# First attention of a four-layer kernel: scores from 32-row operands, and the PSUM banks dealt out anew

## What is computed

```python
h = layernorm(x) * gamma + beta
q, k, v = heads(h @ w_qkv + b_qkv)                  # 16 heads, 8 dimensions each, 1024 tokens, batch of 4
scores = einsum('bhqd,bhkd->bhqk', q, k) / sqrt(8)
attn = softmax(scores, axis=-1)
out = einsum('bhqk,bhkd->bhqd', attn, v)
x = x + (residual + out @ w_out + b_out)
```

## Time and profile before

| what | value |
|---|---|
| median of 3 runs | 2992.23 us (2990.68 to 2992.49) |
| the profiled execution's own time | 2991.15 us |
| its span | 2989.4 us |
| busy share of the span | PE 95%, PE weight load 74%, DVE 78%, ACT 71%, POOL 60% |
| first maxima, first scores, last maxima, last scores start at | 24.1, 60.6, 871.0, 906.7 us |

### The profile page before, as it was taken

The page is one execution under the profiler, slowest core; times in us unless marked ns, Lnnn a source line. Parts: engine busy times, 40 slices in busy tenths (PEclk is TensorE's granted clock), DMA queues, the critical chain, the costliest instruction groups (busy, mean ns, idle before and its releaser), DMA issues.

```text
span 2989.4 us, 46698 instructions
## 1 busy us (share of the span) xinstructions
PE 2852.0 (95%) x16447; PEld 2209.1 (74%) x16447; DVE 2344.6 (78%) x4197; ACT 2124.2 (71%) x4692; POOL 1786.9 (60%) x1312
## 2 busy tenths in 40 slices
PE   6999999999999999999999999999999999999996
PEld 3555555555547777788888888888888888888885
DVE  8878888887777888778787777788777777877776
ACT  3776776777776555677777777777777777787773
POOL 5421521512104555578788787788778788777773
PEclk9999999999999999999999999999999999999997
DMA  1000000000012221000000000000000000000000
GB/s 47 9 16 9 16 9 9 16 9 15 9 49 75 84 84 57 8 1 1 1 1 3 1 3 3 1 3 3 3 1 3 3 1 3 3 1 3 3 3 6
DMA packets 28570, 42.70 MB, mean 14 GB/s; under 512 B 5097, under 2 KB 15913, under 8 KB 28337
## 3 DMA queue, kind: packets, MB, share of 16 engines
q1 hardware_dynamic: 28336, 39.72, 4.6%
HBM read 29.08 MB, written 2.23 MB: 10 GB/s over the span
## 4 chain that ended last, share of the span: by engine, by line
PE 72%; DVE 14%; issue 5%; POOL 5%; ACT 3%; DMA 0%; SPq 0%; DVEq 0%; POOLq 0%; ACTq 0%
PE P L1835 18%; PE P L1676 9%; PE P L1703 8%; PE P L1688 8%; PE P L1862 7%; PE P L1846 6%; PE P L1764 4%; DVE c_nm L1409 4%; DVE c_DT L1434 3%; PE P L1818 3%; PE P L1775 2%; PE P L1872 2%; PE P L1662 2%; POOL d_tn L1105 2%; POOL c_P L2073 2%
## 5 line engine op out<-in xcount | busy, mean ns | idle before, releaser
L1409 DVE TENSOR_REDUCE c_nm<-P 128x1 f32<-128x1024 f32 x512 | 624.3, 1219 | 299.8 <-PE P L1835 297.8
L914 ACT ACTIVATE c_P<-P,c_nm 128x1024 f32<-128x1024 f32 x512 | 573.5, 1120 | 250.9 <-DVE c_nm L1409 246.6
L1233 DVE TENSOR_REDUCE a_mx<-P 128x1 f32<-128x512 f32 x1024 | 641.0, 681 | 120.4 <-PE P L1676 119.7
L790 ACT ACTIVATE a_PT<-P 128x512 f32<-128x512 f32 x1024 | 531.6, 601 | 162.2 <-PE P L1688 160.9
L2073 POOL TENSOR_TENSOR c_P<-c_P,c_P 128x1024 f32<-128x1024 f32 (+1 forms) x256 | 623.1, 2434 | 21.4
L2071 POOL TENSOR_SCALAR c_P<-c_P,c_rr 128x1024 f32<-128x1024 f32 (+1 forms) x256 | 302.2, 1180 | 335.7 <-DVE c_rr L1421 335.7
L1862 PE MATMUL P<-c_DT,c_xkh 128*128 128x256 f32 x2048 | 453.1, 284 | 24.7 <-DVE c_Yl L1442 22.9
L1676 PE MATMUL P<-a_Kp,a_Qs 128*128 128x512 f32 x1024 | 427.5, 422 | 12.9 <-DVE a_mx L1233 5.7
L1688 PE MATMUL P<-a_Qs,a_Kp 128*128 128x512 f32 x1024 | 401.2, 395 | 3.1 <-DMA a_Qs<-a_mT 1.4
L1862 PEld LDWEIGHTS P<-c_DT,c_xkh 128*128 128x128 f32 x2048 | 351.2, 189 | 36.8 <-DVE c_Yl L1442 29.1
L1835 PE MATMUL P<-c_xth,c_Th 128*128 128x512 f32 x1024 | 363.9, 436 | 2.9 <-ACT c_P L914 2.9
(11 more groups left out here) (247 smaller groups left out, 5543.4 us busy)
## 6 DMA issues: line engine op xcount, KB each, us to landing
b_cwB<-cw_scratch SPq DMA_DIRECT2D x64, 256.0 KB, 5.4
a_Kp<-a_Kc SPq DMA_DIRECT2D x60, 128.0 KB, 2.4
c_stg<-in_cw SPq DMA_DIRECT2D x8, 640.0 KB, 4.7
a_Qs<-a_mT SPq DMA_DIRECT2D x256, 2.0 KB
...
```

The lines of the kernel that those rows point to most:

```text
L790: e.activation(m.PT[j][hs % 4][:, :], bank("scores", u, hs, j), ACT.Exp, scale=SCALE).then_inc(m.S["a_exp"])
L914: e.activation(m.P1[s][n % 4][:, :], P[:, k:k + 2, :].rearrange("p c k -> p (c k)"), ACT.Exp, bias=m.nm[:, n % 4, s:s + 1], accum_out=m.sm ...
L1233: e.tensor_reduce(m.mx2[u % 2][:, 16 * (t // 4) + 4 * j + t % 4, half:half + 1], bank("maxima", u, t, j, half), AX, ALU.max).then_inc(m.S[ ...
L1409: e.tensor_reduce(m.nm[:, n % 4, s:s + 1], P[:, k:k + 2, :].rearrange("p c k -> p (c k)"), AX, ALU.max, negate=True).then_inc(m.S["c_nm"])
```

## The change

- `scores` and `maxima` take the 32 partitions of one head alone. `a_Kp` and `a_Kc` become `a_Ks` (128 x 1024, three of them), and `zero`, the 32-row writes and SP's 4 DMAs per unit are gone. Unit 0's keys are written by one 128 x 512 operation each.
- Neighbours in PE's queue are of different heads: maxima go through heads 0, 1, 2, 3 and scores through 2, 3, 0, 1.
- Maxima have banks 0 to 3, with `values`, `divide` and `out_project`, which DVE reads. Scores have banks 5, 6, 7, with `turn_h`, `project`, `row2` and `turn_o`, which ACT reads (`RINGED_ACT`).
- LAG0 is 7: one step of s (8 slots) more between a unit's maxima and its scores.
- Hooks of `row2`, `divide`, `turn_o`, `out_project` and `values` move by 1 to 6 slots. `project` stays.

```diff
-LAG0 = 6
+LAG0 = 7
...
+RINGED_ACT = {"turn_h", "project", "row2", "turn_o"}
...
-    ring = Ring([3, 5, 6, 7])
-    st_ring = Ring([0, 1, 2])
+    ring = Ring([0, 1, 2, 3])
+    act_ring = Ring([5, 6, 7])
...
-        if step[0] in RINGED:
+        if step[0] in RINGED_ACT:
+            p.on([act_ring.take()], *step)
+        elif step[0] in RINGED:
...
-                hook(s0 + 19 + c, 3, "values", b + 1, c)
+                hook(s0 + 19 + c, 7, "values", b + 1, c)
...
-            hook(s0 + 4 + 4 * c, 2, "row2", u, c)
+            hook(s0 + 4 + 4 * c, 3, "row2", u, c)
...
-            hook(e0 + 5 + 4 * r, 1, "divide", u, r)
+            hook(e0 + 5 + 4 * r, 4, "divide", u, r)
             if gr == 3:
-                hook(e0 + 6 + 4 * r, 1, "turn_o", b, r)
-                hook(e0 + 7 + 4 * r, 1, "out_project", b, r)
+                hook(e0 + 6 + 4 * r, 7, "turn_o", b, r)
+                hook(e0 + 7 + 4 * r, 5, "out_project", b, r)
...
+            if um < NU:
+                t, half = (m % 4, m // 4) if um == 0 and m < 8 else (m // 2, m % 2)
+                on_ring("maxima", um, t, i % 4, half)
             if 0 <= ue < NU:
-                p.on([st_ring.take()], "scores", ue, m_e // 4, m_e % 4)
+                p.on([act_ring.take()], "scores", ue, m_e, (i + 2) % 4)
...
-        if wh:
-            w.wait_ge(*v.now("a_z", "project", u, wh, c))
-            for j in range(2):
-                r = slice(32 * j, 32 * j + 32)
-                e.tensor_tensor(m.Kp[0][r, j, cs], m.th[q][r, :], m.tq[q][r, :], ALU.add).then_inc(s)
-        else:
-            e.tensor_tensor(m.Qs[0][:, cs], m.th[q][:, :], m.tq[q][:, :], ALU.add).then_inc(s)
+        e.tensor_tensor((m.Ks if wh else m.Qs)[0][:, cs], m.th[q][:, :], m.tq[q][:, :], ALU.add).then_inc(s)
...
-            w.wait_ge(*at(f"a_kdma{u % 3}", "project", u, 1, 1))
+            w.wait_ge(*at("a_qs", "project", u, 1, half))
...
-        e.matmul(ps, m.Qs[u % 3][:, 128 * t:128 * t + 128], m.Kp[u % 3][:, j, 512 * half:512 * half + 512],
+        e.matmul(ps, m.Qs[u % 3][r, 128 * t:128 * t + 128], m.Ks[u % 3][r, 512 * half:512 * half + 512],
...
-        e.matmul(ps, m.Kp[u % 3][:, j, 128 * kt:128 * kt + 128], m.Qs[u % 3][:, 512 * c:512 * c + 512],
+        e.matmul(ps, m.Ks[u % 3][r, 128 * kt:128 * kt + 128], m.Qs[u % 3][r, 512 * c:512 * c + 512],
...
-            for j in range(4):
-                e.dma_start(m.Kp[u % 3][32 * j:32 * j + 32, j, :].bitcast(F32),
-                            m.Kc[u % 2][32 * j:32 * j + 32, :].bitcast(F32)).then_inc(S[f"a_kdma{u % 3}"], 16)
```

More of the change, by code:

```diff
@@ L136, in project_signals @@
     out = {"a_qk_pe": 1, "a_tq": 1}
-    if u == 0 and w == 1:
-        out |= {"a_first_dve": 4, "a_qs": 2}
-    elif u == 0 and c == 0:
+    if u == 0 and (w == 1 or c == 0):
         out |= {"a_first_dve": 3}
@@ L142, in project_signals @@
         out |= {"a_th": 2, "a_qs": 1}
-    if u and w and c:
-        out[f"a_kdma{u % 3}"] = 64
     return out
@@ L155 @@
 SIGNALS = {
-    "zero": {"a_z": 1},
     "one": {"a_z": 1},
@@ L310, in plan_all @@
         hook(i, 2, "one", i)
-        hook(2 + i, 2, "zero", i + 1)
-    on_ring("project", 0, 1, 0)
-    on_ring("project", 0, 0, 0)
-    on_ring("turn_h", 0, 1)
+    put(("project", 0, 1, 0))
+    put(("project", 0, 0, 0))
+    put(("turn_h", 0, 1))
     hook(0, 4, "project", 0, 1, 1)
@@ L380, in plan_all @@
     p.do("load_cw", 0, 1)
-    ring.slots, ring.i = [7], 0
+    ring.slots, ring.i, act_ring = [7], 0, ring
     pairs = Ring([(0, 1), (2, 3), (4, 5)])
@@ L1232, in maxima @@
             w.wait_ge(*at("a_nm", "row1", u - 2, t // 4))
-        e.tensor_reduce(m.mx2[u % 2][:, 16 * (t // 4) + 4 * j + t % 4, half:half + 1], bank("maxima", u, t, j, half),
+        e.tensor_reduce(m.mx2[u % 2][:, t // 4, j, t % 4, half:half + 1], bank("maxima", u, t, j, half),
                         AX, ALU.max).then_inc(m.S["a_max_dve"])
@@ L2029, in project @@
         q, cs = projects.index((u, wh, c)) % 2, slice(512 * c, 512 * c + 512)
-        if (u, wh) == (0, 1):
-            w.wait_ge(*at("a_first_dve", "project", u, wh, c, i=2))
-            w.wait_ge(*v.now("a_z", "project", u, wh, c))
-            for j in range(2, 4):
-                r = slice(32 * j, 32 * j + 32)
-                e.tensor_tensor(m.Kp[0][r, j, cs], m.th[q][r, :], m.tq[q][r, :], ALU.add).then_inc(m.S["a_qs"])
-        elif (u, c) != (0, 0):
+        if u or (wh, c) == (0, 1):
             w.wait_ge(*at("a_tq", "project", u, wh, c))
@@ L2104, in l_norm @@
                             ALU.pow).then_inc(m.S["d_lnp"])
-    parts = dict(zero=zero, one=one, first=first, ln_gather=ln_gather, ln_apply=ln_apply, residual=residual,
+    parts = dict(one=one, first=first, ln_gather=ln_gather, ln_apply=ln_apply, residual=residual,
                  turn_h=turn_h, project=project, item=item, c_project_low=c_project_low, combine=combine,
```

77 lines of the change are left out of this document (27 added, 50 removed).

## The result

The changed kernel takes 2971.89 us (median of 4, 2967.61 to 2972.89) against 2992.26 for the one before on the same chip: a ratio of 0.993, 95% interval 0.9913 to 0.9947. The direction is as forecast, the size is not. The profiled execution took 2971.69 us.

A forecast was written before the change was run, and what follows sets the result against it. PE was taken as the bound, with eight 128-row matmuls and one `sums` a group. Head 59.9 + 968 x 0.780 + tail 41.2 = 856 for 907, 51 less than 2991.2: 2940 us, range 2850 to 3000.

The forecast's parts named there:

- The ring chain: Plain groups: the fourth score waits for ACT to free the first score's bank; 2.69 us a group for 3.04; chance 0.60.
- The pitch of 32-row matmuls: PE's queue: neighbouring 32-row matmuls start 0.11 us apart; all below 0.17 give the same group.
- Projections, row2 and divide: Groups with extra steps: 3.67 us with a projection, 3.6 with row2 and divide sharing a group.
- the wait on ACT takes back what PE gave: Projection groups: the projection takes a bank of ACT's ring, so the group gains 0.06 us, not 0.35.
- A unit: The 64 slots of a unit take 49.9 us after the change, 0.780 a slot, for 53.1 before.
- the steps of a batch: Steps that a batch has once: 1.1 us a unit for 0.8, since turn_h holds a bank of ACT.
- The tail: Last maxima to last scores: 48 slots become 56, 36.0 + 2 x 2.60 = 41.2 us.
- The head: Start of the stage: the first scores come at 59.9 us for 60.6, with eight further maxima costing 4.8.
- The 3.4 us of the keys' pieces: Head: without the keys' four 32-row pieces, DVE's add for the queries comes 3.4 us sooner.
- the clock falls: Rival, whole stretch: idle PE drops to 1.2 GHz, 1.48 us more a group; a third of it gives 3060; chance 0.07.
- Heads do run side by side: Rival denying this, PE's queue: pitch stays 0.23, plain groups 3.04, only losses count, 3013 us; chance 0.13.
- DVE does not bound: Rival claiming it does, long stretch: 0.647 us a slot, 2811 us; chance 0.17 including times between.

The follow-up runs named there:

- Run 6: The changed kernel with one bank moved: three for maxima, four for scores and the projections, row2 and transposes that share them; 2959.73 us, 0.9903 of before.
- run 8: The changed kernel with the sums of two groups issued back to back every eight slots instead of one every four; 3070.54 us, 1.0273 of before.
- Run 9: The changed kernel with turn_h, project, row2 and turn_o taking banks from the maxima's ring of four; 2964.39 us, 0.9917 of before.
- Run 7: The kernel before, still with 128 rows and a lag of six eighths, given the new bank assignment alone; 2997.83 us, 1.0024 of before.
- run 11: The kernel before with LAG0 at 7 instead of 6 and nothing else; 2994.94 us, 1.0019 of before.
- runs 10: The changed kernel with last unit's scores over 128 rows, DVE's router-weight conversions twelve slots later, GpSimd's residual behind DVE's first projections; 2945.84 us, 0.9854 of before.
- Run 12: Run 10's kernel with unit 0, and unit 1's maxima up to the last 8 slots, over 128 rows; 2938.22 us, 0.9825 of before.
- Run 2: The changed kernel with the last unit's scores alone over 128 rows; 2948.40 us, 0.9865 of before.
- run 5: The changed kernel with GpSimd's first residual adds waiting for DVE's first projection chain; 2969.61 us, 0.9938 of before.
- Run 1: The changed kernel with unit 0's maxima alone again over 128 rows; 2972.84 us, 0.9939 of before.

## Why the prediction was right and wrong

**The ring chain: right.** In plain groups the fourth score waits for ACT's read of the first, released by L782; 2.64 for 2.69. I had put a maxima of 0.10 ahead of the first score, and they start together. Run 6 moved the wait to DVE, and its tail's groups fell to 1.98 with a fourth bank; run 8 gave PE less work and made groups longer. The pitch of 32-row matmuls was taken at 0.11 and is 0.00 to 0.01 between heads, 0.34 on the same rows; as forecast, it did not matter.

**Projections, row2 and divide: right, with one overlap missed.** A projection's group is 3.65 for 3.67. Of a unit's two groups with row2 and divide, one stands by itself and takes 3.65 (I had 3.6). The other falls on a projection's group, which I had not seen, and takes 4.66, 1.01 more than the projection's alone for the 0.9 that I had counted. All in all 4.66 + 3 x 3.65 + 3.65 + 11 x 2.64 = 48.3 against my 10 x 2.69 + 4 x 3.67 + 2 x 3.6 = 48.8. That the wait on ACT takes back what PE gave is right; that it comes of taking a bank of ACT's ring is not. Run 9 gave the projections banks of the other ring and they cost the same, for ACT reads them ahead of the first exponential either way.

**A unit: 49.2 for 49.9, right.** The 0.9 that 48.3 leaves are the steps of a batch, for the 1.1 counted. Run 7 adds what the sum had not split: with 128 rows the new banks by themselves lose 7.4 us, and run 11's lag 6.6. So the gain has to come from the 32 rows; how much they would give on the old banks no run shows.

**The tail: the step that failed.** The term "36.0 + 2 x 2.60 = 41.2" is right at full clock: runs 10 and 12 measure 41.5, run 11 41.3. It took its 2.60 from the earlier trace rows, which are 128-row matmuls, and assumed that 32-row ones keep the clock. They did not: 14 groups at 1.46 more (4.06 - 2.60, where my rival had priced 1.48) are 20 us, and the transposes and small matmuls among them about the rest of 26.6. Run 2 gives 24 us back by widening the last unit's scores to 128 rows.

**The head: failed too.** "First scores at 59.9" came at 67.2. The 3.4 us of the keys' pieces were there, but GpSimd's work, which those pieces had held back, fell on DVE (run 5). I had asked what the memsets and SP's copies cover, and not what GpSimd's own pieces keep apart: the term is right for DVE by itself (first maxima 3.2 earlier in run 5) and puts the collision at nothing without a reason. The clock did the rest: before, it came back at 38 us; with 32-row maxima paced by DVE only at 94. Run 12 puts 7.6 us on it. A smaller reading was off as well: before the change a group with row2 is 3.17, where the prediction has 3.07.

**The rival "the clock falls": right in kind and price, wrong in weight and place.** I gave it 0.07 and set it over the whole stretch. It came at the two ends, a sixth of the stage (22 to 94 and 816 to 890 us), where PE waits most among 32-row work, beside a middle that held. Against it I had set DVE-paced maxima at 42 to 46 us, 128-row matmuls again: the wrong witness, for runs 1 and 12 get the clock back by 38 us on just those, and again within 4 us of a fall at 54, and the changed kernel does not. Whether the rows count by themselves, or by the idle time that shorter work leaves PE, these runs don't part; run 6's tail and the busy 27 us of the head speak against either alone. A rival may be true of a stretch only, and its price belongs in the sum as well as in a chance.

**The other rivals.** Heads do run side by side. DVE does not bound; it idles 0.15 a group. The Trainium skill (TensorE: Matmul & The Clock Gate, "Part 3: Packing small matmuls") was right that four row groups work together, and its rate would have given the same sum. The Trainium skill (TensorEngine Tiling, "Tiling Modes") says that a change of mode drains TensorE. Run 1 agrees, 0.42 to 0.45 a change at full clock, for 0.23 between 128-row matmuls in turn.
